# Four-layer adaLN transformer on one core: throw-away products in the first layer's experts, and two groups of rows moved one step earlier in the third attention

## What is computed

```python
for each layer L:
    sa, ca, ga, sb, cb, gb = silu(c) @ wmod          # ga, gb bounded away from 0
    h = layernorm(x) * (1 + ca) + sa
    x = x + ga * attention_L(h)
    h = layernorm(x) * (1 + cb) + sb
    x = x + gb * ffn_L(h)
```

```python
# ffn of layer 0: a latent attention, then experts
h = h + mla_attention(rmsnorm(h))         # keys and values from a 64-wide normed latent
logits = rmsnorm(h) @ gate.T + gate_b     # 4 experts of 512 hidden units
h = h + sum_e onehot(argmax(logits))_e * (relu(rmsnorm(h) @ W1_e.T + b1_e) @ W2_e.T + b2_e)

# ffn of layer 1 ends, attention of layer 2 begins
x = x + gb * (shared(h) + sum of 4 weighted expert rows of each token)
x = x + ga * causal_attention(layernorm(x) * (1 + ca) + sa)   # 16 heads of 8
```

## Time and profile before

| | us |
|---|---|
| median of 3 runs | 2251.18 (2250.73 to 2251.28) |
| the profiled execution, its own time | 2252.82 |
| its span, first to last instruction | 2250.7 |
| TensorE busy | 1693.2 (75%) |
| VectorE busy | 1546.8 (69%) |
| ScalarE busy | 1110.5 (49%) |
| GpSimd busy | 916.7 (41%) |
| granted TensorE clock, mean over the span | 0.821 |
| first run (passes 0 to 15), from the first maximum to the last expert | ends near 500 |
| third attention's loop | about 1528 to 1713 |

### The profile page before, as it was taken

How to read it: one execution, slowest core, us unless ns; L and a number is a source line. 1 busy time by engine, 2 the same in 40 slices (tenths; PEclk the granted TensorE clock), 3 DMA queues, 4 the chain that set the end, 5 groups by cost and what they waited for, 6 DMA issues and landing times.

```text
span 2250.7 us, 40678 instructions
## 1 busy us (share of the span) xinstructions
PE 1693.2 (75%) x13462; PEld 1276.2 (57%) x13462; DVE 1546.8 (69%) x4926; ACT 1110.5 (49%) x3308; POOL 916.7 (41%) x1256
## 2 busy tenths in 40 slices
PE   4877888884387797797778937735776889999955
PEld 3444666662286686686678626632343367777742
DVE  6778665455778778887776743256676578888667
ACT  2543444438677777777751502211343266666710
POOL 4433212051334334333313446657521066766710
PEclk8988999985586778787688968865796899999967
DMA  4111001011000000000000112223211000000000
GB/s 136 47 43 43 29 19 40 3 48 71 14 8 12 12 9 12 12 10 7 1 1 1 72 29 80 89 76 75 57 34 72 13 1 1 1 2 1 2 1 19
DMA packets 67313, 67.69 MB, mean 30 GB/s; under 512 B 9955, under 2 KB 58966, under 8 KB 66566
## 3 DMA queue, kind: packets, MB, share of 16 engines
q1 hardware_dynamic: 58930, 53.09, 7.2%
q0 software_dynamic: 5120, 10.50, 1.8%
q10 hardware_dynamic: 3040, 1.38, 0.3%
HBM read 30.41 MB, written 8.39 MB: 17 GB/s over the span
## 4 chain that ended last, share of the span: by engine, by line
PE 43%; DVE 21%; issue 9%; POOL 9%; ACT 8%; SPq 7%; another core or an unknown queue 1%; DMA 1%; ACTq 1%; DVEq 0%; POOLq 0%
SPq L673 7%; PE bank L1709 5%; PE bank L1710 5%; PE bank L1723 4%; DVE weights L3007 3%; PE bank L1516 3%; PE bank L1996 2%; PE bank L1532 2%; ACT rope_s L4022 2%; ACT rope_c L4022 2%; PE bank L1860 2%; POOL hid L1120 2%; POOL weights L1144 1%; PE bank L2127 1%
## 5 line engine op out<-in xcount | busy, mean ns | idle before, releaser
L2597 DVE TENSOR_REDUCE nmax<-bank 128x4 f32<-128x1024 f32 x144 | 175.9, 1221 | 73.7 <-PE bank L1305 62.8
L4033 ACT ACTIVATE probsT<-bank 128x512 f32<-128x512 f32 x128 | 75.7, 595 | 187.9 <-PE bank L1710 186.0
L1723 PE MATMUL bank<-V,probsT 128*128 128x9 f32 x1024 | 139.7, 266 | 33.3 <-ACT probsT L4033 33.3
L1723 PEld LDWEIGHTS bank<-V,probsT 128*128 128x128 f32 x1024 | 134.9, 206 | 47.4 <-ACT probsT L4033 38.8
L4168 ACT ACTIVATE big<-bank,nmax 128x256 f32<-128x256 f32 x256 | 119.4, 484 | 52.0 <-DVE nmax L3543 51.9
L875 POOL TENSOR_TENSOR big<-big,rinv 128x512 f32<-128x512 f32 x128 | 132.6, 1050 | 19.1 <-DVE rinv L3549 19.1
L1709 PE MATMUL bank<-const,big 128*128 128x128 f32 x512 | 121.6, 326 | 16.4 <-DVE hid L3060 16.4
L3850 ACT ACTIVATE O<-bank 128x1024 f32<-128x1024 f32 x72 | 73.7, 1023 | 104.8 <-PE bank L1305 75.0
L3850 ACT ACTIVATE feat_o<-bank 128x1024 f32<-128x1024 f32 x72 | 73.7, 1023 | 103.7 <-PE bank L1305 66.1
L2934 DVE TENSOR_REDUCE nmax<-bank 128x2 f32<-128x512 f32 x128 | 85.9, 683 | 52.4 <-PE bank L1694 51.6
L1136 POOL DMA_INDIRECT weights<-h_rows,V x96 | 91.8, 956 | 69.8 <-issue 27.4
(11 more groups left out here) (762 smaller groups left out, 5349.3 us busy)
## 6 DMA issues: line engine op xcount, KB each, us to landing
qT<-parts SPq DMA_DIRECT2D x276, 32.0 KB
big<-V SPq DMA_DIRECT2D x192, 32.0 KB
y_rows<-weights SPq DMA_DIRECT2D x24, 256.0 KB
big<-parts SPq DMA_DIRECT2D x180, 32.0 KB
weights<-in_weights_l_ffn SPq DMA_DIRECT2D x1, 4832.0 KB, 14.1
weights<-in_weights_l_attn SPq DMA_DIRECT2D x1, 3904.0 KB, 12.1
qT<-V SPq DMA_DIRECT2D x96, 32.0 KB
weights<-in_weights_l_ffn SPq DMA_DIRECT2D x1, 2860.0 KB, 11.7
```

The costliest lines, as they stand in the source:

```text
L1723: last = mm(pb[1][:, t * S + h * wide:t * S + (h + 1) * wide], probsT[:, h % 2, at:at + P], values_of(b, k)[:, h * wide:(h + 1) * wide], s ...
L2597: V_.tensor_reduce(to, scored.rearrange("p (i a n) -> p i a n", i=HPG, n=n), AX.X, ALU.max, negate=True).then_inc(score_max.sem, 1)
```

## The change

Three edits.

```diff
             def turn_latent(m):
 
+                pe.wait_ge(value_taken.sem, value_taken(m - 2, 1))
+                keep_warm(pb[6], 8)
                 pe.wait_ge(latent_ready.sem, latent_ready(m, 1))
-                pe.wait_ge(value_taken.sem, value_taken(m - 2, 1))
                 for t in range(T):
                     last = nc.tensor.transpose(pb[6][0:64, t * P:(t + 1) * P], front_n[:, t, 0:64], C("ident"))
...
+            def keep_warm(bank, n):
+
+                for i in range(n):
+                    mm(bank[:, i % 2 * P:(i % 2 + 1) * P], C("ident"), C("ident"), start=True, stop=True)
+
             def turn_post(m):
 
-                pe.wait_ge(post_ready.sem, post_ready(m, 1))
                 if m + 4 <= last_of(m):
                     pe.wait_ge(latent_ready.sem, latent_ready(m + 4, 1))
+                else:
+                    pe.wait_ge(result_taken.sem, result_taken(m, 1))
+                    keep_warm(pb[7], 6)
+                pe.wait_ge(post_ready.sem, post_ready(m, 1))
                 for t in range(T):
                     last = nc.tensor.transpose(pb[7][:, t * P:(t + 1) * P], nb[:, t, :], C("ident"))
...
-                        if k in (2, 3) and ph == "l2_attn" and there(4):
-                            combine(m + 4 - first, (k - 2,))
+                        if k in (1, 2) and ph == "l2_attn" and there(4):
+                            combine(m + 4 - first, (k - 1,))
```

## The result

The kernel after took 2231.94 us (median of 11 runs, 2225.15 to 2246.35), the kernel before beside it on the same chip 2251.21 us (11 runs, 2245.25 to 2268.11). The ratio is 0.9897 with a 95% interval of 0.9876 to 0.9918: about 23 us faster (18.5 to 27.9), by the sum of the prediction it was to be 12.6. The profiled execution took 2229.91 us, its span is 2228.1.

The account below looks back on a forecast made before the run. No engine was full: TensorE, at half clock in first rises, bounded the experts; VectorE's maximum, with GpSimd close behind, the third attention. Products -7.4 and moved rows -5.2 gave -12.6: 2238.6 us from 2251.18, range about 2231 to 2247.

Parts of the forecast that it names:

- The filler products, -7.4 us: First layer's experts: throw-away products in TensorE's gaps keep its clock up for the first `rise`; -7.4 us net.
- six of seven held, -8.7: Passes 8 to 14: the clock stays up at six of seven first rises, 10.1 x 6/7 = -8.7 us.
- the 10.1 of the prediction's rows: Passes 8 to 14: first rises of 24.03 us in all fall to 13.93 us if all hold, 10.1 us.
- Pass 14's transpose, +1.3: Pass 14's other transpose has no gap worth filling, so six products delay it, with nothing to hide this; +1.3 us.
- Passes 8 to 11, cover enough, 0: Experts: the transpose comes 0.6 us later four times, covered by TensorE's later wait for GpSimd; 0, without cover 2.4 us.
- The moved rows, -5.2: Third attention's loop: `combine` rows moved ahead of `split_qk` take 1.25 instead of 3.65 us, shortening TensorE's waits; -5.2 us.
- n = 0: Third attention's loop: GpSimd has no slack before `split_max(m, 1)` of n = 1, and the later intake costs +0.4 us.
- n = -1: Third attention's loop: step 2 gets late beside `split_qk`, costing +0.7 us.
- `result_piped` beside `split_qk`, 0.3 us: Third attention: two additions and a multiplication now lie beside GpSimd's `split_qk`, costing 0.3 us in an iteration bound by GpSimd.
- its second figure for n = 3, -0.6 us: Third attention: if two instructions each waited 1.15 us for GpSimd, -2.9 us would shrink to -0.6 us.
- GpSimd did become the bound of the third attention: Rival: GpSimd keeps the third attention, so the moved rows bring about 0; 2243.8 us, chance 0.17.
- a late start at half clock: Rival: the experts' filler products start at half clock and delay the transposes; +9 us, 2260 us, chance 0.04.

Follow-up runs that it names:

- e16: The kernel after, unchanged, measured again on another chip; ratio to before 0.9896 (0.9871 to 0.9922).
- e1: The kernel after with the third attention's moved combine rows put back, so the throw-away products alone; ratio to before 0.9926 (0.9901 to 0.9951).
- e3: The kernel after, unchanged, for a second trace; one run, 2193.17 us.
- e6: The kernel after with thirteen more copies of a small VectorE operation ahead of layer 1's attention; ratio to before 0.9924 (0.9897 to 0.9951).
- e15: The kernel after with five more copies of a small VectorE operation ahead of layer 1's attention; ratio to before 0.9911 (0.9882 to 0.9940).
- e2: The kernel before with only the third attention's combine rows moved; ratio to before 0.9979 (0.9961 to 0.9998).
- e4: The kernel before, unchanged, for a second trace; one run, 2217.13 us.
- e5: The kernel before with five more copies of a small VectorE operation ahead of layer 1's attention; ratio to before 0.9991 (0.9973 to 1.0008).
- e13: The kernel before with seven more copies of a small VectorE operation ahead of layer 1's attention; ratio to before 0.9957 (0.9940 to 0.9973).
- e14: The kernel before with nine more copies of a small VectorE operation ahead of layer 1's attention; ratio to before 0.9990 (0.9966 to 1.0014).
- e7: The kernel after with 4 and 3 throw-away products in place of 8 and 6; ratio to before 0.9901 (0.9874 to 0.9928).
- e12: e7 with seven more products in the idle stretch ahead of the next attention's first transposes; ratio to before 0.9912 (0.9890 to 0.9934).
- e9: The kernel after with only the eight products ahead of `turn_latent`, without those of the last four passes' `turn_post`; ratio to before 0.9932 (0.9909 to 0.9956).
- e10: The kernel after with only the six products of the last four passes' `turn_post`, without those ahead of `turn_latent`; ratio to before 0.9951 (0.9929 to 0.9973).
- e11: The kernel after with 2 and 1 throw-away products in place of 8 and 6; ratio to before 0.9932 (0.9909 to 0.9956).

## Why the prediction was wrong

The direction and both mechanisms were right, the size was not: 2238.6 us was given with a range down to about 2231; by the ratio it is about 2228. The median itself is 2231.94 us; the ratio of e16 speaks for the larger gain. That the forecast came this near is in part luck, since it left out a stage that gave about as much as each of its own terms.

- **The filler products, -7.4 us (six of seven held, -8.7, and +1.3)**: the mechanism was right, the size was 10.1 by the means. All seven held. Against before's spread, the six traces with the full products (after, e1, e3, e6, e15, e16, the deliberate delay taken off) have the experts at -13.9, -12.2, -12.2, -12.2, -10.0 and -15.4, mean -12.7; the six without any (before, e2, e4, e5, e13, e14) 0, -3.5, -3.2, +2.6, -5.9 and -5.5, mean -2.6. The products are worth 10.1 us there, with some 3 us of doubt, which just holds the 7.4 forecast. That it equals the 10.1 of the prediction's rows is luck. Those rows came from a trace in which all seven first rises were slow; over the six traces without products the seven take 22.7 us in the mean, 8.7 more than 7 x 1.99, since pass 14's was at full clock in four of the six and pass 13's too in two. The rest came from stretches that the sum did not count: in the mean some 42 us of the stage are at 0.50 without the products and 20 us with them. The 13.9 of the first pair of traces is too high by the same scatter.
- **Pass 14's transpose, +1.3**: right in kind, 0.9 us in size, and it is inside the 10.1. e13 and e14 had the clock up in this pass without any product, and there pass 14's first rise begins 28.1 us behind pass 13's; with six products (after, e1, e3, e16) it is 29.0 us, with three (e7, e12) 28.3. First e13, then after:

```profile
446.10 0.44 PE L1495 MATMUL bank<-const,nb 128*128 128x128 f32 x2 [0.43 <-DVE nb L2500]
```

```profile
435.65 1.60 PE L1493 MATMUL bank<-const 128*128 128x128 f32 x12
437.09 0.38 PE L1504 MATMUL bank<-const,nb 128*128 128x128 f32 x2
```

- **"Passes 8 to 11, cover enough, 0"**: right, up to 237.7 us after is 1.5 us ahead, other traces with the full or half products are 0.1 to 2.7 ahead and before's second trace 1.6.
- **The step that failed** is the one that wasn't taken: the sum ends with the two stages that the change touches. The first attention, 497 us of untouched code, was put at nothing without a reason. It became shorter: with the products and no added delay it was -7.6, -7.6, -7.7 and -4.2 us, without either 0, -0.3 and +3.1, by the means 7.7 us, with 3 to 4 us of doubt. Its length goes with where the clock's changes fall against its work: e6 lost the gain by a delay and e13 found it by one, with none of the products. That it fell to the change's favour is luck: nothing in the change aimed at it, and with other numbers of products (e9 +6.7, e10 +0.1) it did not.
- **The moved rows, -5.2**: right on the kind of chip it was forecast for, nearly term by term. Intervals between the starts of `split_max(m, 1)`, after less before, from the rows above and the earlier trace rows: n = 0 (1552.41 to 1573.68, now 1533.09 to 1555.56) +1.2 where +0.4 was forecast; n = 1 -1.9 (-1.7); n = 2 -1.75 (-1.7); n = 3 -2.8 (-2.9). Ahead of them n = -1 costs 0.7 us, as forecast: after is 20.0 us ahead at 1533 us and 19.3 at the first of these instructions. From 1533 to 1646 us the eight traces with the moved rows on the slower kind of chip are 3.4 to 5.5 us shorter than before's, e5 without them is 2.0 longer. On the faster kind the difference is smaller: 11.6 to 13.9 us shorter with them (e2, e3, e15, e16), 10.6 to 11.7 without (e1, e4, e13, e14), 1.3 by the means. e2's rounds, on that kind, say 4.6 us (0.4 to 8.7).
- **"`result_piped` beside `split_qk`, 0.3 us"**: 0.3 us for each of two instructions, 0.6 in an iteration. GpSimd in the kernel after, beside the two that begin at 1570.27 and 1571.05 us:

```profile
1569.58 1.16 POOL L958 TENSOR_TENSOR weights<-weights,parts 128x512 f32<-128x512 f32 x1
1570.80 0.69 POOL L959 CAST parts<-weights 128x512 bf16<-128x512 f32 x1
```

  When each of the two began, 0.47 and 0.44 us of GpSimd's instruction were left, and 0.3 us was lost. The Trainium skill (SBUF — State Buffer, Who interferes with whom) says that whoever comes first keeps the shared ports for its whole instruction and blocks the other; that is at most what is left of the instruction, and so read the rows agree with it. The prediction reckoned with the whole of it, 1.15 us twice; so its second figure for n = 3, -0.6 us, was far from the -2.8 measured.

By terms: -10.1 - 7.7 - 4.6 = -22.4 us, against the measured -23.2 (18.5 to 27.9). Each of the three has 3 to 4 us of doubt, so it is partly luck that they meet so closely.

Of the rivals none came. The fillers hold the clock at the first rises; GpSimd did become the bound of the third attention, as the forecast had it for n = 0, but the rows paid all the same; a late start at half clock did not occur. The range was too narrow because it held only the uncertainty of the two edits, while one and the same kernel's runs lie 21 us apart (2225 to 2246).

## What to carry to other kernels

Filling a wait with throw-away products pays where the gap is followed at once by a burst of TensorE that bounds the stage, and here half of the products gave the same time, though not in every trace the same clock; more products than the gap holds cost what they overhang. Before pricing any change to such a kernel, ask how long the stages that it does not touch are when they start a microsecond earlier or later: here delays of 0 to 1.6 us on one and the same kernel moved one stage by 14.5 us (+3.1 in e4, -11.4 in e13), more than either edit. A gain of under 0.5% then needs a second trace of each kernel and a control that only adds a delay.

## What was not expected of the hardware

- One microsecond of useless work ahead of a stage of 497 us made it 11.4 us shorter (e13). Length and granted clock belong together: 497.3 us at 0.78, 489.7 at 0.79 (after), 485.8 at 0.80.
- On one and the same kernel 0.5 us of added delay gave -0.4 in that stage (e5, first 1.00 at 14.1 us) and 1.0 us gave -11.4 (e13, at 13.3 us); 1.6 us gave -5.0 (e14, at 12.9 us).
- Four products of throw-away work (0.9 us at 0.233 us each) in a gap that stays idle for another 1.24 us kept the clock at 1.00 in all seven passes of one trace (e7) and in five of seven of another (e12), by the same instructions with the same gaps; two of them did in four of seven (e11).
- The time that the experts spend at 0.50 differs between executions of one program: 47.8 and 41.0 us (before, e4), 13.7, 24.1 and 6.8 us (after, e3, e16), and the stage's length goes with it: 0, -3.2, -13.9, -12.2 and -15.4 us.
- Chips of this type differ by 1.8% on the same kernel (2216 to 2257 us), 28 to 29 us of it in one stretch of layer 1's ffn. Why was not tried.
